# A two-layer graph, mixing and expert kernel: the experts' second biases, early attention weights, and graph products amid the edge counting

## What is computed

```
xn = LN(x)
# layer 0: graph convolution, three steps, then linear attention, both on xn
out_deg = max(count(src), 1); in_deg = max(count(dst), 1)
g = xn
for i in 0..2:
    g = (g - mean(g)) * rsqrt(var(g) + EPS) * gamma[i] + beta[i]
    h = g * out_deg ** -0.5
    g = relu((segment_sum(h[src], dst) * in_deg ** -0.5) @ W[i] + b[i])
x = x + g + mix0(xn)
# layer 0 experts: 16 routed, top 4 of a softmax, 2 shared
t = LN(x)
x = x + sum_e combine[:, e] * (gelu(t @ re_w1[e] + re_b1[e]) @ re_w2[e] + re_b2[e])
      + sum_j (gelu(t @ se_w1[j] + se_b1[j]) @ se_w2[j] + se_b2[j]) / 2
# layer 1: two graph attention convolutions with 4 heads of 256, then a linear part
xn = LN(x)
a = relu(gat(xn, W1, b1)); a = relu(gat(a, W2, b2))
x = x + a @ Wfc + bfc + mix1(xn)
# layer 1 experts: 16 routed, top 2, 1 shared, SwiGLU with learned clamps
t = LN(x)
x = x + sum_e combine[:, e] * (swiglu5(t @ expert_w1[e] + expert_b1[e]) @ expert_w2[e] + expert_b2[e])
      + (swiglu5(t @ shared_w1 + shared_b1) @ shared_w2 + shared_b2)
```

## Time and profile before

| | |
|---|---|
| median of three executions | 2422.84 us |
| the profiled execution's own time | 2420.39 us |
| its span | 2417.9 us |
| granted TensorE clock, mean | 0.97 |
| TensorE busy | 2183.7 us, 90% |
| VectorE busy | 1001.3 us, 41% |
| ScalarE busy | 511.2 us, 21% |
| GpSimd busy | 287.1 us, 12% |
| moved by DMA | 154.57 MB |

### The profile page before, as it was taken

The page is one execution under the profiler, slowest core; times in us unless marked ns, Lnnn a source line. Parts: engine busy times, 40 slices in busy tenths (PEclk is TensorE's granted clock), DMA queues, the critical chain, the costliest instruction groups (busy, mean ns, idle before and its releaser), DMA issues. The chain is left out here.

```text
span 2417.9 us, 26622 instructions
## 1 busy us (share of the span) xinstructions
PE 2183.7 (90%) x7344; PEld 1247.0 (52%) x7345; DVE 1001.3 (41%) x2721; ACT 511.2 (21%) x903; POOL 287.1 (12%) x317
## 2 busy tenths in 40 slices
PE   6998879999998988884998989979989989989997
PEld 3444434545455444443543468854468854535554
DVE  7957875302115522122033465512165412734543
ACT  1112221011103022222210144301154202301111
POOL 1200000000000044453210000000000010003333
PEclk9999999999999999997999999989999989999999
DMA  4003000000003257677001000020000010347774
GB/s 122 1 0 115 1 1 18 1 18 0 0 1 125 65 124 172 149 173 178 5 1 43 18 1 1 1 95 1 0 1 1 1 39 26 106 152 222 236 238 107
DMA packets 77185, 154.57 MB, mean 64 GB/s; under 512 B 10201, under 2 KB 21508, under 8 KB 77100
## 3 DMA queue, kind: packets, MB, share of 16 engines
q1 hardware_dynamic: 59436, 113.06, 14.1%
q0 software_dynamic: 17664, 40.43, 8.5%
HBM read 119.50 MB, written 36.18 MB: 64 GB/s over the span
## 5 line engine op out<-in xcount | busy, mean ns | idle before, releaser
L1849 PE MATMUL bank<-arena 125*125 125x257 f32 x1600 | 354.5, 382 | 4.7 <-DVE arena L1768 4.7
L1849 PEld LDWEIGHTS bank<-arena 125*125 125x125 f32 x1600 | 301.3, 188 | 60.1 <-DVE arena L1768 6.3
L2099 PE MATMUL bank<-arena 128*128 x832 | 257.5, 444 | 16.0 <-issue 8.8
L950 PE MATMUL bank<-arena 125*128 125x500 f32 (+1 forms) x720 | 253.0, 512 | 2.3 <-ACT arena L970 2.3
L1664 PE MATMUL bank<-arena 128*125 128x512 f32 x480 | 209.9, 597 | 8.9 <-DMA arena<-in_L_gnn_W 8.9
L478 PE MATMUL bank<-arena 128*125 128x512 f32 x480 | 213.7, 594 | 2.1 <-PEq L318 1.1
L2099 PEld LDWEIGHTS bank<-arena 128*128 128x128 f32 x832 | 152.0, 192 | 111.2 <-issue 61.3
L2119 PE MATMUL bank<-arena 128*128 x360 | 181.2, 611 | 25.0 <-issue 16.6
L950 PEld LDWEIGHTS bank<-arena 125*128 125x128 f32 x720 | 135.6, 189 | 120.1 <-issue 110.1
L2217 DVE TENSOR_TENSOR arena<-bank,arena 128x384 f32<-128x384 f32 (+1 forms) x104 | 51.7, 497 | 279.7 <-PE bank L2099 270.1
L1827 ACT ACTIVATE arena<-arena 125x625 f32<-125x625 f32 x160 | 134.5, 902 | 102.4 <-DVE arena L1768 102.2
(11 more groups left out here) (326 smaller groups left out, 2237.5 us busy)
## 6 DMA issues: line engine op xcount, KB each, us to landing
arena<-in_L_ffn_expert_w SPq DMA_DIRECT2D x16, 1536.0 KB
arena<-in_L_ffn_re_w SPq DMA_DIRECT2D x32, 512.0 KB, 8.2
arena<-in_L_ffn_expert_w SPq DMA_DIRECT2D x16, 768.0 KB
arena<-in_L_mix_Wqkv SPq DMA_DIRECT2D x6, 1024.0 KB, 16.3
arena<-in_L_ffn_expert_b SPq DMA_DIRECT2D x16, 384.0 KB
token_rows<-arena SPq DMA_DIRECT2D x2, 2500.0 KB
arena<-in_L_gnn_W SPq DMA_DIRECT2D x1, 4096.0 KB, 13.0
arena<-in_L_gnn_W SPq DMA_DIRECT2D x3, 1024.0 KB, 5.5
```

Of the source, the lines that this page charges most:

```text
L950: last = pe.matmul(st.bank[4 + n % 4][:, 0:cn], h[:, s, f * P:(f + 1) * P], st.counts[:, s, c0:c0 + cn], start=(s == 0), stop=(s == NT - 1))
L1849: return pe.matmul(st.bank[n % OUTS][0:TS, 0:ONCOL], prob[:, u % 2, s, j * TS:(j + 1) * TS], st.slots[:, head + 1, s, :], start=(s == 0), ...
L2099: last = pe.matmul(st.bank[UP[b][h]][:, 0:WP], xt[b][:, k, :], rt.ring[:, bass.ds(r, 1), k * W + h * WP:k * W + (h + 1) * WP].rearrange("p ...
```

## The change

1. **Graph products amid the counting.** `EARLY_TILES = 7`: the 28 matmuls of the first seven tiles of h of step 0 are made by TensorE at the ends of the counting windows (one per window, two at three of them) into banks 4 to 7, and copied by ScalarE unscaled. In `stage_graph` VectorE scales these seven, TensorE makes the other three. The sum over the sources comes after that, in three pieces, and the three spread matmuls after the second and third aggregate. The out-degree parts are summed after windows 5, 10, 15, 20 and 23, the last two windows' columns by one reduction of VectorE.
2. **Shared second bias.** It is loaded as a broadcast, scaled on VectorE ahead of the chain of places (`own_bias`; layer 0 also adds its two shared biases), and added to `res3` by GpSimd in ten additions.
3. **Routed second bias.** The matmul by the combine weights goes, with the transposes and copies. Each expert's second bias is loaded as a broadcast of 128 rows of 2 KB (256 KB) behind its w2; VectorE adds it to each tile's rows (`bias_last`), from the bank into a new buffer from which ScalarE weighs. The bank and the ring slot are free when that addition is done. Layer 0 loads two experts ahead of the loop, not three.
4. **Attention weights.** W1 is loaded in `stage_mix` of layer 1, the first half of W2 in the first `stage_attend`, its second half at the start of the second `stage_project`, whose first tile multiplies by the first halves first; Wfc in the second `stage_attend`.

```diff
@@ stage_adjacency
+    SUMMED = [5, 10, 15, 20, 23]
...
+            dve.wait_ge(counts_placed, NW)
+            dve.tensor_reduce(parts[:, :, 5:6], st.counts[:, :, SUMMED[-1] * WIN:], AX_X, ALU.add).then_inc(part_summed, 1)
...
+            steps = [(t, k) for t in range(EARLY_TILES) for k in range(KT)]
+            def early_products(w):
+                for t, k in steps[w * len(steps) // NW:(w + 1) * len(steps) // NW]:
+                    if t == 0 and k == 0:
+                        pe.wait_ge(st.graph_w_loaded, 16)
+                        pe.wait_ge(x_ready, KT)
+                    if k == 0 and t >= 4:
+                        pe.wait_ge(st.early_placed, t - 3)
+                    last = pe.matmul(st.bank[BANKS + t % 4][0:TS, :], st.turned[:, k, t * TS:(t + 1) * TS],
+                                     st.graph_w[:, k, :], start=(k == 0), stop=(k == KT - 1))
+                    if k == KT - 1:
+                        last.then_inc(made, 1)
...
+                    early_products(w)
...
+                while placed < EARLY_TILES and w * KT * EARLY_TILES // NW >= KT * (placed + 1):
+                    act.wait_ge(made, placed + 1)
+                    act.copy(st.early_h[placed], st.bank[BANKS + placed % 4][0:TS, :]).then_inc(st.early_placed, 1)
+                    placed += 1
@@ stage_graph
+    SPREAD_AFTER = {1: (0, 1), 2: (2,)}
...
+            for s in range(EARLY_TILES):
+                dve.tensor_scalar(h[s], h[s], src_norm[:, s:s + 1], None, ALU.mult).then_inc(early_scaled, 1)
...
-                    dve.tensor_reduce(by_target, st.counts.rearrange("p s n -> p n s"), AX_X,
-                                      ALU.add).then_inc(targets_summed, 1)
+                    for c, (c0, cn) in enumerate(CHUNKS):
+                        dve.tensor_reduce(by_target[:, c0:c0 + cn], st.counts[:, :, c0:c0 + cn].rearrange("p s n -> p n s"),
+                                          AX_X, ALU.add).then_inc(targets_summed, 1)
...
-                for s in range(NT):
+                for s in range(0 if i else EARLY_TILES, NT):
...
-                    if i == 0 and s == NT - 3:
-                        pe.wait_ge(targets_summed, 1)
-                        for c, (c0, cn) in enumerate(CHUNKS):
-                            pe.matmul(st.bank[4 + c][:, 0:cn], st.ones[0:TS, :], by_target[:, c0:c0 + cn],
-                                      start=True, stop=True).then_inc(row_spread, 1)
...
+                    if i == 0 and n in SPREAD_AFTER:
+                        for d in SPREAD_AFTER[n]:
+                            d0, dn = CHUNKS[d]
+                            pe.wait_ge(targets_summed, d + 1)
+                            pe.matmul(st.bank[d][:, 0:dn], st.ones[0:TS, :], by_target[:, d0:d0 + dn],
+                                      start=True, stop=True).then_inc(row_spread, 1)
@@ class L0_EXPERTS, load_expert
-    slots, early = P, 3
+    slots, early = P, 2
...
+        sp.wait_ge(rt.w2_loaded, 32 * e)
     sp.dma_start(w2, ins[kind.w2][e].rearrange("(f p) n -> p f n", p=P)).then_inc(rt.w2_loaded, 16)
+    sp.dma_start(b2, ins[kind.b2][e].unsqueeze(0).to_broadcast([P, D])).then_inc(rt.w2_loaded, 16)
@@ stage_front
+                sp.dma_start(bias_rows[:, n, :], sb2[n].unsqueeze(0).to_broadcast([TS, D])).then_inc(bias_loaded, 16)
...
+            pool.wait_ge(bias_step, kind.shared)
+            for t in range(NT):
+                pool.tensor_tensor(st.res3[:, t, :], st.res3[:, t, :], bias_rows[:, 0, :], ALU.add).then_inc(res_biased, 1)
...
-                if m == COMBINE_AFTER:
-                    pe.wait_ge(comb_ready, 1)
-                    pe.wait_ge(shared_set, 1)
-                    pe.wait_ge(counts_used, 1)
-                    for t in range(NT):
-                        c, at = t // 4, (t % 4) * TS
-                        last = pe.transpose(st.bank[COMBINE[c]][0:total, at:at + TS], comb[:, t, :], st.ident[0:TS, 0:TS])
-                    last.then_inc(comb_turned, 1)
...
-                pe.matmul(bank[0:TS, :], comb_t[:, t * TS:(t + 1) * TS], b2,
-                          start=False, stop=True).then_inc(down_ready, 1)
+                        last = pe.matmul(bank[0:TS, :], hid[n][:, f, t * TS:(t + 1) * TS], w2[n][:, f, :],
+                                         start=(n == 0 and f == 0), stop=(n == kind.shared - 1 and f == F - 1))
+                last.then_inc(down_ready, 1)
...
-            def place_combine():
-                act.wait_ge(comb_turned, 1)
-                for c, (c0, cn) in enumerate(CHUNKS):
-                    act.activation(comb_t[:, c0:c0 + cn], st.bank[COMBINE[c]][0:total, 0:cn], ACT.Copy,
-                                   scale=1.0 / kind.shared_weight).then_inc(comb_placed, 1)
...
+            def own_bias():
+                dve.wait_ge(bias_loaded, 16 * kind.shared)
+                if kind.shared == 2:
+                    dve.tensor_tensor(bias_rows[:, 0, :], bias_rows[:, 0, :], bias_rows[:, 1, :], ALU.add).then_inc(bias_step, 1)
+                    dve.wait_ge(bias_step, 1)
+                dve.tensor_scalar(bias_rows[:, 0, :], bias_rows[:, 0, :], kind.shared_weight, None, ALU.mult).then_inc(bias_step, 1)
...
+            own_bias()
             find_places(dve)
...
+            dve.wait_ge(res_biased, NT)
@@ early_weights, stage_project, stage_attend
+    ew.load = [load(0, ew.wide, ins["L1_gnn_W1"]), load(1, ew.wide, ins["L1_gnn_W2"][0:KT * P, :]),
+               load(2, ew.linear, ins["L1_gnn_Wfc"])]
...
-            sp.dma_start(w, weight.rearrange("(k p) n -> p k n", p=P)).then_inc(w_loaded, 16)
+            if layer == 1:
+                sp.dma_start(late, weight[KT * P:K * P, :].rearrange("(k p) n -> p k n", p=P)).then_inc(w_loaded, 16)
...
+            def product(t, half, ks):
+                n = 2 * t + half
+                if n >= 4 and ks[0] == 0:
+                    pe.wait_ge(half_placed, n - 3)
+                for k in ks:
+                    x = st.turned[:, k, t * TS:(t + 1) * TS] if layer == 0 else gt[:, t % 2, k, :]
+                    w = ew.wide[:, k] if k < KT else late[:, k - KT]
+                    last = pe.matmul(st.bank[n % 4][0:TS, :], x, w[:, half * 512:(half + 1) * 512],
+                                     start=(k == 0), stop=(k == K - 1))
+                if ks[-1] == K - 1:
+                    last.then_inc(half_ready, 1)
...
+                if layer == 1 and t == 0:
+                    for ks in (range(KT), range(KT, K)):
+                        if ks[0]:
+                            pe.wait_ge(w_loaded, 16)
+                        for half in range(2):
+                            product(t, half, ks)
+                else:
+                    for half in range(2):
+                        product(t, half, range(K))
...
+        block.sync(load)
...
-            sp.dma_start(w, weight.rearrange("(k p) n -> p k n", p=P)).then_inc(w_loaded, 16)
@@ stage_routed
-                    sp.wait_ge(down_ready, sp.value_load(rt.done_by[0:1, e - R:e - R + 1], min_val=1, max_val=TILES + 1))
+                    sp.wait_ge(y_biased, sp.value_load(rt.done_by[0:1, e - R:e - R + 1], min_val=2, max_val=TILES + 2))
...
-                pe.wait_ge(y_made, g + 1)
+                pe.wait_ge(w2_loaded, e * 32 + 32)
+                pe.wait_ge(y_biased, g + 1)
...
-                act.wait_ge(down_ready, g + 2)
-                act.activation(y[b], st.bank[DOWN[b]], ACT.Copy, scale=weight[:, bass.ds(g, 1)]).then_inc(y_made, 1)
+                act.wait_ge(y_biased, g + 3)
+                act.activation(y[b], whole_y[b], ACT.Copy, scale=weight[:, bass.ds(g, 1)]).then_inc(y_made, 1)
...
+            def bias_last(g, b):
+                r = ring_of(dve, g)
+                dve.wait_ge(down_ready, g + 2)
+                dve.wait_ge(y_made, g + 1)
+                dve.tensor_tensor(whole_y[b], st.bank[DOWN[b]],
+                                  rt.ring[:, bass.ds(r, 1), B2_AT:B2_AT + D].rearrange("p a n -> p (a n)"),
+                                  ALU.add).then_inc(y_biased, 1)
...
+                    bias_last(g - 1, 1 - b)
...
+            bias_last(g - 1, 0)
+            bias_last(g, 1)
@@ main
+        stage_mix(nc, st, free, mw, ins["L1_mix_bproj"], ins["L1_mix_temperature"], ew.load[0])
+        stage_attention(nc, st, Arena(whole, DYN, words), ins, ew)
```

146 lines of the change are left out of this document (78 added, 68 removed).

## The result

| | before | after |
|---|---|---|
| median of the runs, us | 2424.78 (2420.90 to 2428.79, 4 runs) | 2402.56 (2399.18 to 2404.07, 4 runs) |
| ratio | | 0.9906, 95% interval 0.9885 to 0.9927 |
| profiled execution, its span | 2420.39, 2417.9 | 2404.07, 2402.3 |

What follows compares the result with a forecast made beforehand. TensorE, busy 90%, bounds most stages, but not layer 0's routed loop, where GpSimd waits for scatter-adds. Terms −11.5 −4.6 +17.7 −35.2 −12.4 +7.8 = −38.2 from 2420.4 give 2382.2, plus 2.4: median 2384.6 us, range 2364 to 2408.

Steps and rivals of the forecast that it cites:

- Counting: Counting of edges: products at window ends add 15 us, TensorE's first graph product then starts 2.0 earlier; stage +13.0.
- Graph, −24.5: Graph layers: first aggregate 11.3 us after the first product, not 38.96; a new stall of 1.1; in all −24.5 us.
- Front of layer 0, −4.6: Layer 0's expert front: ten transposes and a matmul go, but TensorE stalls 6.7 us behind VectorE's chain; −4.6 us.
- rival (a): Both fronts: GpSimd's additions hold VectorE's chain, +6.5 us in layer 0, +3 in layer 1; median 2394; chance 0.28.
- Loop of layer 0, +17.7: Layer 0's routed loop: longer load costs 1.2 us for each of 14 experts, VectorE's addition only 0.9; +17.7 us.
- scatter-adds beside a load about 11 us apart: Sign of the forecast in the changed kernel's profile; 12.5 us under (b), 9.8 under (c), 14 to 15 under (d).
- (c): Rival: the loop doesn't notice the longer load, +0.9 us instead of +17.7; 2368 us; chance 0.12.
- (b): Rival: the longer load costs 2.8 us per expert instead of 1.2, +22 us; 2407 us; chance 0.13.
- (d): Rival: the scatter-add waits for the whole bias broadcast, 5.15 us, in the loop, +55 us; 2440 us; chance 0.05.
- Attention, −35.2: Starts of the attention parts: earlier loads remove TensorE's waits for weights and slow starts, −35.2 us; waits alone −29.7.
- Front of layer 1, −12.4: Layer 1's expert front: removed TensorE work saves 13.5 us, a wait behind VectorE's chain costs 1.1; −12.4 us.
- Loop of layer 1, +7.8: Layer 1's routed loop: later slot release lengthens two load waits by 2.9 us each, last tile's chain by 2.0; +7.8.

Runs made afterwards that it cites:

- e5: Changed kernel with the shared bias loaded first, then summed, scaled and added by GpSimd, nothing of it on VectorE; 2396.56 us, 0.9882 of the kernel before.
- e4: Changed kernel without the load of the routed second bias; VectorE adds the first 512 words of w2 instead; 2394.01 us, 0.9885 of the kernel before.
- e6: Changed kernel with the routed second bias loaded but not added, bank and slot released as before; 2386.55 us, 0.9841 of the kernel before.
- e7: Changed kernel where SP waits only for the product before loading w1, b1, w2, and for the addition before the second bias; 2395.39 us, 0.9886 of before.

## Why the prediction was right or wrong

**Counting, +13 forecast, +11.0 measured: right.** Up to the opening of the last window it takes 14.3 us more (forecast +15 for the products): most of the first twenty windows take 5.67 us for 5.05, so a product costs 0.62 there, and the four after them take what they took (8.38 for 8.39, then 5.85 to 5.91 for 5.88 to 5.90), so those hide, as forecast. The end, from there to the first product of the graph layers, is 3.4 shorter, not 2.0.

**Graph, −24.5, measured −24.7: right**, each of its steps: first aggregate at 11.31 (11.3), stall 0.73 (1.1). VectorE's scaling of the early tiles took 0.41 us a tile, not 0.55, and was never waited for.

**Front of layer 0, −4.6, measured +3.2: wrong, and rival (a) came true.** The step that failed is that "GpSimd's ten additions, 10 × 1.18, are covered by the 37 us of VectorE's chain". They lie beside it, and the chain got 7.9 us longer by them; rival (a) gave +6.5, and its 13 us of stall came as 8.25 and 4.15. e5, which moves the additions off the chain of places (and onto the top k), gives 6.9 back. The fall to the low clock after the stall, 1.7 in the forecast, is there too (3.91 for 2.26 us of matmuls). The Trainium skill, SBUF — State Buffer, § Who interferes with whom, whose rule the prediction set against the change, agrees with the rows: operations with two SBUF inputs were held (1.20 for 0.17), those with one in PSUM weren't (0.20 as before). It also says what the prediction left out, that copies can enter a mode that takes both port pairs and are then held too, and that a reduction never is; the copies of 2, 4 and 8 columns took 1.19, that of one column 0.15, the reduction 0.32.

**Loop of layer 0, +17.7, measured +23.1: the size nearly right, by wrong steps.** The step that failed is that "VectorE's new addition" and its buffer "lie beside GpSimd's chain and cost nothing but 0.9 us in the last tile": alone the addition costs 10 to 15 us (e4), as it stands ahead of the release of the ring slot and so of the next load. I had priced the transfer by its bytes and never drawn the cycle that issues it. The load was priced at 1.2 us per expert, and alone it costs just this in the first half of the period, 12.3 for 11.1 (e6); but in the change, beside the addition, it is worth 0.2 to 0.6 per expert (3 to 8 us). So the sign that the prediction had named, scatter-adds beside a load about 11 us apart, didn't come: they stand 9.3 apart, as under (c), and 10.4 in e6. The price of (b), 2.8, and that of (d) appear in no run, and (c), nothing, is out by e6. That the sum stayed near is luck: one cost was left out, and the one that was counted shrank beside it. The fourteenth expert's load in the loop was counted for its second bias alone; what its own 1.125 MB cost there is not known.

**Attention, −35.2, measured −33.6: right**; all three waits went, the second half of W2 landed in time.

**Front of layer 1, −12.4, measured −7.1: wrong by the same hold.** Rival (a) gave +3 here, and +5.3 came: the stall is 4.49 at ScalarE's SwiGLU, which starts only when VectorE is through its held chain (ScalarE's wait of 11.09).

**Loop of layer 1, +7.8, measured +14.1: right in kind, mis-sized.** The term is "grow by 2.9 each": the two one-tile waits, each read with its idle stretch, went from 9.5 and 9.3 to 16.6 and 13.1 us a tile, 7.1 and 3.8 more. The addition stands on VectorE behind SwiGLU's work. e7, which takes this wait off w1, b1 and w2, gives 7.4 of it back, e6 13.3. "VectorE's addition fills its idle 1 us per tile" was no cover for it.

So the sum missed by 7.8 + 5.3 in the fronts and 5.4 + 6.3 in the loops; the rest of the forecast stands within 2 us per stage. By the medians the forecast is 18.0 us too low. Rival (a)'s time, 2394, is nearer than the forecast's 2384.6, and holds for the fronts alone; (b)'s 2407 is nearer still, by a mechanism that no run shows.

## What to carry to other kernels

When a change adds work ahead of what frees a buffer of a ring, draw the cycle from the load's issue to the next issue and price the work there, not on the engine that is idle; and look which part of the buffer is free sooner: here the early release of one part was worth 35 us, about as much as the attention weights. An engine's idle time is no cover either for an operation that can hold another engine's critical chain (ten additions of 1.24 us on GpSimd made VectorE's 7.9 us longer); compare the operands of both engines in the same stretch of the timeline before you place it.

## What the runs showed of the hardware

- Beside GpSimd additions of 125x512 (1.24 us each), even one-input VectorE copies of 125x2 to 125x8 within SBUF took 1.19 us, for 0.17 otherwise. Seven operations of 2 to 16 columns took a whole GpSimd addition each, however small they are, so with the two ahead of them the chain lost 7.9 us. Operations of 160 columns took up to 1.34 for 0.33 beside them (e5); the reductions (0.32) and those that read PSUM (0.20) took what they took.
- A scatter-add beside an expert's load started 9.2 us after the one ahead of it, and 6.3 when w1 was issued earlier and w2 7 us behind it. With 256 KB more in the load, in the broadcast form, the way from issue to that scatter-add grew from 11.1 to 12.3 us in e6, and from 10.7 to 11.2 where VectorE's addition stood in the cycle (e4 and the change).
- Loops of identical code took 301.1 to 306.6 and 264.9 to 271.3 us in four kernels that differ only outside them, and 319.6 to 324.2 and 279.0 to 284.8 in four others. Not explained.
